# A new order for the end of an attention and feed-forward kernel, and a weighted sum moved by one burst in every attention step

## The reference, cut to what matters

```python
Q = split_heads(x, 16)                    # no projection of Q; 16 heads of 16
K = split_heads(x @ Wk + bk, 16)
V = split_heads(x @ Wv + bv, 16)          # 1024 columns, 64 per head
scores = Q @ K.T + causal_mask
attn = softmax(scores)
o = (attn @ V).transpose(0, 2, 1, 3).reshape(B, S, -1)
a = x + gelu(o) @ Wf + bf
x = layernorm(x + a)
h = silu(x @ wg.T / 127) * (x @ wu.T / 127)      # wg, wu, wd are integers; 768 hidden
x = layernorm(x + h @ wd.T / 127)
```

## Time and profile before

| | us |
|---|---|
| median of three runs | 1818.3 |
| lowest and highest | 1817.98 and 1820.29 |
| the profiled execution | 1819.79 |
| its span, first to last instruction | 1818.1 |
| TensorE (PE) busy | 1758.2 (97%) |
| VectorE (DVE) busy | 1376.3 (76%) |
| GpSimd (POOL) busy | 1242.5 (68%) |
| ScalarE (ACT) busy | 1052.8 (58%) |

### The profile page before, as it was taken

How to read it: one execution, slowest core, us unless ns; L and a number is a source line. 1 busy time by engine, 2 the same in 40 slices (tenths; PEclk the granted TensorE clock), 3 DMA queues, 4 the chain that set the end, 5 groups by cost and what they waited for, 6 DMA issues and landing times. The chain is left out here.

```text
span 1818.1 us, 37771 instructions
## 1 busy us (share of the span) xinstructions
PE 1758.2 (97%) x10340; PEld 965.1 (53%) x10340; DVE 1376.3 (76%) x3417; ACT 1052.8 (58%) x1375; POOL 1242.5 (68%) x1137
## 2 busy tenths in 40 slices
PE   7999999999999999999999999999989999999996
PEld 5545444444444444444444444343466767676763
DVE  5777777777777777777778777787568787878874
ACT  2465665666666566665666666556645555555552
POOL 3598999989999998999989899878313131212121
PEclk9999999999999999999999999999999999999998
DMA  9676657556565655646656555564586666767500
GB/s 317 174 230 176 177 154 201 159 166 190 146 179 179 163 165 169 189 142 194 173 146 197 154 171 149 141 182 116 143 215 154 189 158 186 160 181 165 176 22 24
DMA packets 261153, 303.17 MB, mean 167 GB/s; under 512 B 28240, under 2 KB 177872, under 8 KB 261072
## 3 DMA queue, kind: packets, MB, share of 16 engines
q1 hardware_dynamic: 261072, 302.19, 59.0%
HBM read 174.20 MB, written 127.93 MB: 166 GB/s over the span
## 5 line engine op out<-in xcount | busy, mean ns | idle before, releaser
L1183 ACT ACTIVATE weights<-ring 128x1024 f32<-128x1024 f32 x576 | 572.8, 1027 | 190.3 <-PE ring L858 187.1
L813 POOL TENSOR_TENSOR weight_sum<-weight_sum,weights 128x512 f32<-128x512 f32 (+2 forms) x371 | 551.2, 1486 | 48.5 <-POOL weight_sum L792 8.6
L858 PE MATMUL o_acc<-weights,v_pair 128*64 128x512 f32 (+3 forms) x3072 | 583.2, 500 | 0.7 <-POOL weights L762 0.6
L849 POOL TENSOR_TENSOR h_lo<-hidden,h_hi 128x512 f16<-128x512 f32 x96 | 114.4, 1193 | 394.3 <-ACT h_hi L1117 394.3
L1334 DVE TENSOR_REDUCE part_max<-ring 128x2 f32<-128x1024 f32 x256 | 301.2, 1218 | 69.7 <-PE ring L858 69.7
L858 PEld LDWEIGHTS o_acc<-weights,v_pair 128*64 128x64 f32 x3072 | 187.3, 136 | 291.5 <-issue 239.4
L1343 DVE CUSTOM_DVE_ANT_0 scrap<-ring,causal 128x128 bf16<-128x128 f32 (+3 forms) x512 | 224.7, 486 | 116.5 <-PE ring L858 116.1
L858 PE MATMUL ring<-q_stack,k_stack 50*128 50x512 f32 (+3 forms) x1536 | 262.8, 380 | 19.6 <-DVE part_max L1334 12.5
L1343 DVE CUSTOM_DVE_ANT_0 scrap<-ring,causal,part_max 128x256 bf16<-128x256 f32 (+3 forms) x512 | 251.2, 546 | 29.3 <-PE ring L858 26.2
L858 PE MATMUL ring<-k_stack,q_stack 48*128 48x512 f32 (+3 forms) x1536 | 256.7, 372 | 0.6 <-DMA k_stack<-k_rows 0.5
L858 PE MATMUL ring<-wf_sb,g 128*128 128x256 f32 x1024 | 230.7, 380 | 2.9 <-ACT g L1204 1.8
(11 more groups left out here) (128 smaller groups left out, 2218.9 us busy)
## 6 DMA issues: line engine op xcount, KB each, us to landing
v_pairs<-v_unit SPq DMA_DIRECT2D x64, 512.0 KB, 3.5
v_pair<-v_pairs SPq DMA_DIRECT2D x64, 512.0 KB, 5.1
o_heads<-o_pair SPq DMA_DIRECT2D x64, 512.0 KB, 3.4
g<-o_heads SPq DMA_DIRECT2D x16, 2048.0 KB, 8.2
den_wide<-reciprocals SPq DMA_DIRECT2D x32, 1024.0 KB, 13.5
q_stack<-q_rows SPq DMA_DIRECT2D x128, 192.0 KB, 3.6
k_stack<-k_rows SPq DMA_DIRECT2D x128, 192.0 KB, 4.3
q_rows<-x_hi SPq DMA_DIRECT2D x28, 512.0 KB, 3.6
```

Source lines behind the costliest of these rows:

```text
L813: pool.tensor_tensor(dst, other, weights(t), ALU.add).then_inc(s_add, 1)
L849: pool.tensor_tensor(h_lo[:, f], h32[f % 2][:], h_hi[:, f], ALU.subtract).then_inc(s_hl, 1)
L858: return nc.tensor.matmul(o, l, r, start=start, stop=stop)
L1183: nc.scalar.activation(W[i][:], bank_of("t", i)[:], ACT.Exp).then_inc(s_w, 1)
```

## The change

1. Group 5's weighted sum moves from b = 4 to b = 5, for all pairs.
2. ScalarE in b = 4 does T6's exponential ahead of the copy of o's first half.
3. The diagonal block is copied into acc0 by ScalarE (`copy_diagonal`, end of b = 1) and no longer by GpSimd. GpSimd adds group 3 straight behind group 1, ahead of `begin_sum`.
4. APART becomes PAIRS - 10. The two last pairs' sums on VectorE get a semaphore of their own (s_half) and the order 1, 3, 2.
5. In r = 66 the tiles of the first unit's product come in b = 1, 2, 3, 4, behind the weighted sums and the denominators of their burst.
6. SP loads g of unit 1 at r = 64, between the stores of o and of the denominators.
7. `finish(0)` on VectorE multiplies unit 1 ahead of the additions to unit 0.

```diff
-        ADDS = (1, 10, 2, 3, 7, 9, 11)
+        ADDS = (1, 3, 10, 2, 7, 9, 11)
-        APART = PAIRS - 9
+        APART = PAIRS - 10
+        ENDING = PAIRS - LEAD
+        EARLY_SUMS = (1, 3, 2)
...
                     store_o(r - 3, n - 3)
+                    if r == PAIRS:
+                        sp.wait_ge(s_wrest, 3)
+                        load_g(1, 0)
                     store_den(r - 3, n - 3)
...
-                if r == PAIRS + 1:
-                    sp.wait_ge(s_wrest, 3)
-                    load_g(1, 0)
...
-                if i == 0:
-                    if rt >= 2:
-                        pool.wait_ge(s_den, n - 1)
-                        settle(pool, s_passed["pool"])
-                    pool.affine_select(out=acc0[rt % 2][:, :, 0:P], in_=W[0][:, :, 0:P], compare_op=ALU.is_ge, fill=0.0,
-                                       base=0, pattern=[[0, 2], [1, P]], channel_multiplier=-1)
...
+                if t == 1 and rt >= 2:
+                    pool.wait_ge(s_den, n - 1)
...
                     if r < PAIRS:
                         add(1, *m)
+                        add(3, *m)
                     begin_sum(*m)
                     add(10, *m)
                     if r < PAIRS:
                         add(2, *m)
-                        add(3, *m)
...
+                if rn >= ENDING:
+                    pe.wait_ge(s_half, len(EARLY_SUMS) * (rn - ENDING + 1))
+                pe.wait_ge(s_add0, n + 1)
...
-                        back, at = after(r, b, NBURST * LEAD + lag)
+                        back, at = after(r, b, NBURST * LEAD + lag + (t == 5))
                         if 0 <= back < PAIRS and at == 0:
                             weigh(t, r, back, n + back - r, it)
-                    if r == PAIRS + LEAD and b == 0:
-                        pe.wait_ge(s_wrest, 3)
-                        pe.wait_ge(s_w, NU * (PAIRS - 1) + 7)
-                        wf_product(0, 0, (0,))
-                    if r == PAIRS + LEAD and b in (1, 3, 4):
-                        wf_product(0, 0, (max(b - 1, 1),))
                     back, at = after(r, b, NBURST * LEAD + DEN_AT)
                     if 0 <= back < PAIRS and at == 0:
                         denominators(back, n + back - r)
+                    if r == PAIRS + LEAD and b == 1:
+                        pe.wait_ge(s_wrest, 3)
+                        pe.wait_ge(s_w, NU * (PAIRS - 1) + 7)
+                    if r == PAIRS + LEAD and 1 <= b <= UT:
+                        wf_product(0, 0, (b - 1,))
...
+            def copy_diagonal(rt, n):
+                act.wait_ge(s_sel, NM * n + masked(0))
+                if rt >= 2:
+                    act.wait_ge(s_den, n - 1)
+                copy(acc0[rt % 2][:, :, 0:P], W[0][:, :, 0:P]).then_inc(s_add0, 1)
...
-                    if 0 <= back < PAIRS and at == 0:
-                        copy_o(0, back, n + back - r, it)
+                    half_done, at = after(r, b, NBURST * LEAD + O0_AT)
+                    copied = not (0 <= half_done < PAIRS and at == 0)
                     for what, i in uses(b):
                         if what == "t" and LEAD <= r < PAIRS + LEAD:
                             exponent(i, r - LEAD, n - LEAD)
+                        if not copied:
+                            copy_o(0, half_done, n + half_done - r, it)
+                            copied = True
+                    if b == 1 and LEAD <= r < PAIRS + LEAD:
+                        copy_diagonal(r - LEAD, n - LEAD)
...
-                for t in (1, 2, 3):
+                for k, t in enumerate(EARLY_SUMS):
...
-                    dve.wait_ge(s_add, sums(rt, n, t) - 1)
+                    dve.wait_ge(s_den, n - 1)
+                    if k:
+                        dve.wait_ge(s_half, len(EARLY_SUMS) * (rt - ENDING) + k)
...
                         dve.wait_ge(s_yn, UT * n)
+                    else:
+                        norm(1, it, range(HC))
                     add_x((0, 1))
...
-                elif r + 1 < UNITS:
-                    norm(r + 1, it, range(HC))
```

More of the change, by code:

```diff
@@ L290, in build @@
         s_pv = sem("weights_used")
+        s_add0 = sem("diagonal_block_copied")
         s_add1 = sem("sums_begun")
         s_add = sem("sums_made")
+        s_half = sem("first_half_sums_made")
         s_add8 = sem("last_sum_made")
@@ L391, in s_width @@
             return min(BANK, P * (u + 1) - BANK * kc)
-        ADDS = (1, 10, 2, 3, 7, 9, 11)
+        ADDS = (1, 3, 10, 2, 7, 9, 11)
         NA = len(ADDS)
-        APART = PAIRS - 9
+        APART = PAIRS - 10
+        ENDING = PAIRS - LEAD
+        EARLY_SUMS = (1, 3, 2)
         def sums(rt, n, t=None):
-            made = NA * n - max(rt - APART, 0)
+            made = NA * n - max(rt - APART, 0) - len(EARLY_SUMS) * max(rt - ENDING, 0)
             if t is None:
                 return made
-            return made + ADDS.index(t) + 1 - (rt >= APART and ADDS.index(t) > ADDS.index(7))
+            order = [i for i in ADDS if not (i == 7 and rt >= APART or i in EARLY_SUMS and rt >= ENDING)]
+            return made + order.index(t) + 1
         STEPS_B = PAIRS + 5
@@ L1180, in exponent @@
                         act.wait_ge(s_den, n)
+                    elif i < use_of(4) and rt > ENDING:
+                        act.wait_ge(s_half, len(EARLY_SUMS) * (rt - ENDING))
+                        if i == use_of(10):
+                            act.wait_ge(s_add, sums(rt - 1, n - 1, 10))
                     else:
@@ L1225, in attend @@
                         copy_den(back, n + back - r, it)
-                    back, at = after(r, b, NBURST * LEAD + O0_AT)
-                    if 0 <= back < PAIRS and at == 0:
-                        copy_o(0, back, n + back - r, it)
+                    half_done, at = after(r, b, NBURST * LEAD + O0_AT)
+                    copied = not (0 <= half_done < PAIRS and at == 0)
                     for what, i in uses(b):
@@ L1375, in first_half_sum @@
                     dve.wait_ge(s_sel, NM * n + masked(t))
-                    dve.wait_ge(s_add, sums(rt, n, t) - 1)
+                    dve.wait_ge(s_den, n - 1)
+                    if k:
+                        dve.wait_ge(s_half, len(EARLY_SUMS) * (rt - ENDING) + k)
                     v.tensor_tensor(dst, W[0][:, :, BANK - w:BANK] if t == 1 else dst, weights(t), ALU.add
-                                    ).then_inc(s_add, 1)
+                                    ).then_inc(s_half, 1)
             def reciprocals(i, first):
```

## The result

The changed kernel takes 1823.8 us (median of ten runs, 1823.15 to 1825.0) against 1818.3 us before (ten runs): ratio 1.003, 95% interval 1.0021 to 1.004. It is slower by 0.3%, where I had forecast 1822. The profiled execution took 1823.15 us with a span of 1821.4, 3.3 us more than before's span; the medians differ by 5.5. What follows accounts for the 3.3 of the two profiles.

The account below looks back on a forecast made before the run. TensorE was taken to bound the kernel, busy 77.78 of 78.40 us a period. The terms 16 + 9 - 8 - 5 - 3 - 5 = +4 us gave 1822 on the median of 1818.3; range 1804 to 1831.

Parts of the forecast that it names:

- part 3: Eight steps without projection (r = 56 to 63): waits at T0, T1, T4 go, S8's takes back 0.5: -5 us.
- part 5: End of attention: VectorE's and TensorE's waits for unit 2 both end 5 us sooner: -5 us, bounds -2 and -7.
- Part 1: Fifth burst: TensorE waits for ScalarE at S8 in odd steps, +16 us, and at the projection in even steps, +9.
- Rival A: Odd steps: ScalarE's chain does not bind, S8 finds its bank free, the 16 us fall away: 1806; chance 0.30.
- Part 2: Steady steps, GpSimd relieved of the diagonal copy: T4's wait at r mod 4 = 0 goes, -8 us.
- Part 4: Boundary for group 7 one pair earlier: the long step falls from 20.5 to 17.5 us, -3 us.
- Rival B: End doesn't pay, g of unit 2 keeps its landing, next step's maxima late as before: 1831; chance 0.14.
- C: Whole kernel: new waits take the place of old ones, gains at the end are cancelled: 1818; chance 0.14.
- Costed at nothing: Last two pairs: three sums given to VectorE, no longer chained to GpSimd's, were taken as worth 0.

Follow-up runs that it names:

- e1: Changed kernel with group 5's weighted sum back in b = 4 and the copy of o's first half back ahead of T6's exponential: 1802.1 us, ratio 0.991.
- e4: Changed kernel, but in steps without a projection in b = 4 ScalarE copies o's first half behind both exponentials: 1807.5 us, ratio 0.9943.
- e8: e1 with the diagonal block's copy back on GpSimd and group 3's addition back behind group 2's: 1807.0 us, ratio 0.9925.
- e7: e1 with ScalarE's copy of the diagonal block behind x_high instead of ahead of it: 1800.3 us, ratio 0.9889.
- e6: Changed kernel with group 5's move and the copy behind both exponentials only from r = 56 on, earlier steps as before the change: 1798.6 us, ratio 0.9885.
- e10: e1 with the boundary from which group 7 goes to TensorE back at PAIRS - 9: 1805.2 us, ratio 0.9921.
- e11: e1 with the first unit's product tiles back in b = 0, 1, 3, 4, ahead of weighted sums and denominators: 1810.3 us, ratio 0.9949.
- e12: e1 with the load of g of unit 1 back at r = 65 and VectorE's multiplication of unit 1 behind the first additions: 1806.1 us, ratio 0.9923.
- e2: Changed kernel with only group 5's weighted sum back in b = 4: 1802.5 us, ratio 0.9919.
- e3: Changed kernel with only ScalarE's order undone, copy of o's first half and then both exponentials: 1818.7 us, ratio 1.0.
- e9: e6 and e7 together: 1796.1 us, ratio 0.9866.

## Why the forecast held, step by step

The forecast of 1822 was right in sign and size, and its sum for the steady part (+17) met +17.15. But two terms of that sum were off against one another, and so were part 3 and part 5.

**Part 1** (forecast 25 us: odd steps 16, even 9). Right in place and mechanism; 0.6 us was split otherwise than I had it, though: not 0.5 of idle time and 0.1 for the restart, but 0.33 of idle time in a step that is 0.66 longer. After against e1, step by step: odd steps +0.66 and +0.43 us, 14.7 over the 54 steps (13.5 periods); even steps +0.31 and +0.21, 7.0. The whole stretch gives 20.3 (1075.94 - 1055.67). The term was some 5 us too large: 0.6 us is right for r mod 4 = 3, while both r mod 4 = 1 and r mod 4 = 0 lose less. For r mod 4 = 1 the waits give a reason that no run isolates: from r = 2 to 55 e1 waits there 19 times, 6.6 us, for the maxima, after only 13 times, 5.1 us, so the wait at S8 takes the place of others. Rival A (the chain does not bind) is refuted by the 35 waits and by e4.

**Part 2** (forecast -8). The wait at r mod 4 = 0 went, and that step gained 0.61 us (e8 to e1), the 0.6 of the forecast. What failed is the sentence that "the next step's 0.26 us wait stays": it grows. GpSimd's x_low there waits for x_high, which is behind ScalarE's new copy, and the step r mod 4 = 1 loses 0.42. Net 0.23 us a period, -3 us in all. e7 shows most of the cause: with the copy behind x_high that step gets 0.31 of the 0.42 back. I had costed that ordering as GpSimd's gain eaten, when it is a loss. A second wait had no term in part 2: ahead of `add(7)` GpSimd now stands some 0.9 us a step until VectorE has added group 6, which the kernel before does not show. What that costs was not isolated. GpSimd's group in e1, 460 to 1100 us:

```profile
L814 POOL TENSOR_TENSOR weight_sum<-weight_sum,weights 128x1024 f32<-128x1024 f32 x33 | 78.6, 2381 | 31.7 <-DVE weight_sum L1379 31.0 <-POOL weight_sum L814 0.2
```

**Part 3** (forecast -5, in r = 56 to 63). This step failed; the six from r = 58 gave +0.4. The waits at T0 and T1 did go, as forecast, but I had one claimant for the freed time (S8's wait, 0.5) and there were two. Timeline of VectorE and TensorE in after, a step without projections: the last sum, the maxima, T4 and S8.

```profile
1188.93 1.32 DVE L1387 TENSOR_TENSOR weight_sum<-weight_sum,weights 128x1024 f32<-128x1024 f32 x1
1190.17 2.34 DVE L1353 TENSOR_REDUCE part_max<-ring 128x2 f32<-128x1024 f32 x2
...
1192.57 0.50 PE L859 MATMUL ring<-q_stack,k_stack 50*128 50x512 f32 x2 [0.22 <-DVE part_max L1353]
...
1201.28 0.49 PE L859 MATMUL ring<-k_stack,q_stack 48*128 48x512 f32 x2 [0.23 <-ACT weights L1190]
```

VectorE waits for nobody here: it goes from S0's maxima into the last sum and the next maxima, back to back, and T4 still waits 0.22 us for it. "With GpSimd earlier that at T4 goes" assumed that GpSimd still set VectorE's time. Taking the wait at S8 away prices both sides: with the copy out of the chain (e4, e6) these steps fall from 17.56 to 16.97 us. So the wait costs 0.59, near the 0.5 of the forecast, and what failed is the gain of 1.1 from T0, T1 and T4, of which the runs show 0.5 (17.50 to 16.97).

**Part 4** (forecast -3). r = 56 and 57 gave -3.15, of it 3.05 in r = 57 (20.49 to 17.44); e10 puts the boundary alone at 2.4. Inside the bounds.

**Part 5** (forecast -5, lower bound -7; measured -8.2). The times up to unit 1's product came as forecast. From the last exponential's start, forecast and measured: the denominators at +12.4 and +12.1, unit 1's multiplication done at +19.4 and +18.7, its product at +22.4 and +22.0. TensorE resumes at +40.5 instead of +46.65, 6.1 us sooner where I had said 5. The gate was the right one: the load of den_wide for unit 2 leaves 6.0 us sooner (+17.2 instead of +23.1), since the denominators do; my own numbers had 5.6 there (1307.64 to 1302), of which I carried on only 5. The bound of -2 did not hold: g of unit 2 is held until unit 0's last y_pre (done at 1323.04) and is issued only 2.7 us sooner, but that cost nothing, since it then lands in 17.1 us instead of 20.5. In before, after, e1, e11 and e12 g lands 21.0 to 22.1 us behind den_wide's issue, though it is issued anywhere from 1.5 to 4.9 us behind it. SP's row for g before, then den_wide and g in after:

```profile
1314.31 1.43 SPq L641 DMA_DIRECT2D g<-o_heads  x1
```

```profile
1318.30 1.30 SPq L659 DMA_DIRECT2D den_wide<-reciprocals  x2
1323.14 0.39 SPq L646 DMA_DIRECT2D g<-o_heads  x1
```

Of the remaining 2 us the clock behind the resume, which I had kept for the bound of -7, explains some 1.4 by estimate: it is 1.00 in after (window 1341 to 1345), where before it was 0.66 over the 4 us from 1336.2, and a third of 4 us is 1.4. The rest is within what single profiles differ by: from the resume to the end e1, with a clock of 1.00 behind it too, takes 481.4 us, after 479.8 and before 481.8.

```profile
1313.21 1.07 PE L859 MATMUL o_acc<-weight_sum,ones 128*32 128x512 f32 x8
...
1323.09 7.17 PE L859 MATMUL ring<-wf_sb,g 128*128 128x256 f32 x32 [0.85 <-DVE y_pre L1459]
...
1341.65 0.39 PE L859 MATMUL o_acc<-y_hi,wg_sb 128*128 128x512 f16 x1 [1.88 <-DVE hidden L1490]
```

The fence above is TensorE's timeline in after, to be held against the earlier trace rows. Rival B (the end doesn't pay) is refuted by it, C by the steady part's +17.

**Costed at nothing:** the last two steps of attention became 2.0 us shorter. e8 gives 1 us of that back (28.11 against 27.14 us from r = 64 to the last exponential). The other 1 us is the moved sum's: the stretch takes 27.14 and 27.13 us in e1 and e2, where the sum is back, and 26.12 in e3, where only the copy's order is.

So the answer was right partly by luck: -3 where I had -8 and 20 where I had 25 in the steady part, 0 for -4 in the steps behind it, and -10 for -5 at the end.

## What to carry to other kernels

Work moved out from ahead of a product in a ring of buffers costs its engine nothing and still costs time, if the engine that frees the buffer runs a chain with no gap in it: find the chain's end and compare it with the new arrival, step by step. Restrict such a move to the steps where it pays (here those without projections, e6), and put a copy that can go anywhere behind whatever somebody waits for, which may differ from step to step. When an instruction is given to another engine, look not only for idle time there but for what is queued behind it and whom that feeds: 0.42 us of 0.61 came back, 0.31 of it through x_high and x_low. And an engine that is given less work may spend the time waiting for another, as GpSimd does ahead of `add(7)`.

## What the runs showed of the hardware

- **The clock behind a wait.** Waits of TensorE of 5.41 us (e11) and 3.09 us (e12) at the same product were followed by 4 us at a granted clock of 0.50, that is 1.2 GHz throughout. Waits of 1.88 (after), 1.86 (e1) and 2.09 us (e8) at that product were followed by 1.00, 2.4 GHz; waits of 2.16 (e7), 2.44 (e9) and 2.47 us (e3) by 0.59, 0.57 and 0.60 over 4 us. Among e1 to e10 these three are also the profiles with the longest ends, 523.3 to 523.4 us against 520.4 to 521.9. In e10 two waits of 1.32 and 0.39 us within 1.5 us lie in a window with 0.79. So the length of one wait is not all that decides, and what a shortened wait is worth may be more than its own length. e8, then e7:

```profile
1324.70:1328.70 4.00, 3.97 (x19) 1.85 (x20) 3.82 (x5) 2.05 (x4) 2.00 (x2) 1.00 1.06 207
```

```profile
1317.20:1321.20 4.00, 4.00 (x12) 1.45 (x13) 2.81 (x4) 1.66 (x3) 1.15 (x1) 0.59 1.06 205
```

- **GpSimd's short additions beside VectorE.** I had cited a rule (the Trainium skill, GPSIMD Engine Reference, specifications: the two share their SBUF interfaces when VectorE reads two inputs from SBUF) that no row showed. Now rows do. In the groups of GpSimd's instructions, 460 to 1100 us, before and then after, the 128x256 additions fell from 1065 to 730 ns in the mean; in e8, with the old order and the copy on GpSimd, the mean is 1060 again, in e1 733. The 1065 is a mean of two lengths with nothing between: 25 of the 65 began while VectorE was adding two tiles, and these took 1.54 to 1.62 us; the other 40 took 0.73 to 0.74. The 128x512 additions part in the same way, 8 at 2.3 us and 58 at 1.3. So what lengthens one is to start behind VectorE's addition. The group before, then VectorE's addition and such a one of GpSimd:

```profile
L813 POOL TENSOR_TENSOR weight_sum<-weight_sum,weights 128x256 f32<-128x256 f32 x65 | 69.2, 1065 | 5.7 <-POOL weight_sum L813 0.4
```

```profile
525.30 1.29 DVE L1362 TENSOR_TENSOR weight_sum<-weight_sum,weights 128x1024 f32<-128x1024 f32 x1
525.58 1.60 POOL L813 TENSOR_TENSOR weight_sum<-weight_sum,weights 128x256 f32<-128x256 f32 x1
```

  In after the 128x512 masks rose from 639 to 691 ns in the mean, because 8 of the 97 now begin inside such an addition and take 1.3 us, twice their length.

- **A small store behind large loads.** The denominators' store kept SP waiting 1.1 us in e1 and 3.9 us in e12, where den_wide's load was on its way: a store of 8 KB held up the next load of 2 MB by 2.8 us.
- **A load behind another.** g (2 MB), issued 1.6 us behind den_wide (2 MB) in before, landed after 20.5 us; issued 4.8 us behind it in after, it landed after 17.1: 22.1 and 21.9 us from den_wide's issue. So in these traces den_wide's issue, and not g's own, set when g landed.
- **The new copy itself** took 410 ns (128x256 from SBUF on ScalarE, mean of 64), where I had interpolated 0.4 us.
